# Layer 1 experts: the loads of an expert wait for the adds of the expert eight places ahead of it

## What is computed

```
logits = x @ gate_w.T;  probs = softmax(logits);  4 experts of 32 are picked per token
buf[e, slot] = x[token]                       # up to 256 rows for each of 32 experts
gu = buf @ w_gate_up[e]                       # (256 x 256) @ (256 x 256)
expert_out = (silu(g) * u) @ w_down[e]        # (256 x 128) @ (128 x 256)
routed[token] += expert_out[e, slot] * gate   # scatter-add, 256 rows per expert
out = x + tanh(g_ffn) * (routed + shared expert)
```

## Time and profile before

| | us |
|---|---|
| median of the runs | 1098.03 |
| the profiled execution | 1095.2 |
| its span | 1093.2 |
| TensorE matmul busy | 909.6 |
| GpSimd busy | 541.6 |
| first add instruction of the stage starts | 922.30 |
| last add instruction of the stage starts | 1050.72 |

### The profile page before, as it was taken

The page is one execution under the profiler, slowest core; times in us unless marked ns, Lnnn a source line. Parts: engine busy times, 40 slices in busy tenths (PEclk is TensorE's granted clock), DMA queues, the critical chain, the costliest instruction groups (busy, mean ns, idle before and its releaser), DMA issues. The chain is left out here.

```text
span 1093.2 us, 18614 instructions
## 1 busy us (share of the span) xinstructions
PE 909.6 (83%) x5465; PEld 764.5 (70%) x5465; DVE 663.3 (61%) x2223; ACT 459.7 (42%) x1721; POOL 541.6 (50%) x592
## 2 busy tenths in 40 slices
PE   4998759999999698888538999999999979999920
PEld 3673437787877487777437888998898866888710
DVE  4603035777777466565438899999999963444431
ACT  1313652322322135544326577777777741222200
POOL 1300123455555625555534765565556553677861
PEclk8878988888988699999869999999999989999965
DMA  9521884668776967676499963623413004999689
GB/s 307 185 91 49 246 237 126 161 189 226 237 207 197 248 205 220 213 244 208 130 267 199 222 162 102 230 77 127 136 40 111 12 16 135 264 256 241 70 192 156
DMA packets 163957, 189.71 MB, mean 174 GB/s; under 512 B 16035, under 2 KB 145209, under 8 KB 163858
## 3 DMA queue, kind: packets, MB, share of 16 engines
q1 hardware_dynamic: 112882, 121.87, 38.1%
q0 software_dynamic: 33792, 46.46, 19.7%
q10 hardware_dynamic: 17184, 20.19, 5.4%
HBM read 96.19 MB, written 103.63 MB: 183 GB/s over the span
## 5 line engine op out<-in xcount | busy, mean ns | idle before, releaser
L1794 ACT ACTIVATE att<-bank,mx 128x77 f32<-128x77 f32 x512 | 160.2, 355 | 18.8 <-DVE mx L1875 17.2
L1742 POOL DMA_INDIRECT slots_d<-rows,place x128 | 130.1, 1017 | 71.8 <-DVE place L1963 40.9
L1794 ACT ACTIVATION_READ_ACCUMULATOR att<-bank,mx 128x1 f32 x512 | 121.3, 237 | 0.0
L960 POOL DMA_INDIRECT y_d<-rows,targets x78 | 80.9, 1037 | 70.5 <-DVE rows L1291 47.3
L2061 PE MATMUL bank<-vwo_hi,attT_hi 128*128 128x256 f32 x320 | 94.3, 295 | 3.0 <-DMA vwo_lo<-vwo_lo_d 2.0
L2062 PE MATMUL bank<-vwo_lo,attT_hi 128*128 128x256 f32 x320 | 91.4, 286 | 0.0
L2063 PE MATMUL bank<-vwo_hi,attT_lo 128*128 128x256 f32 x320 | 91.1, 285 | 0.0
L2061 PE MATMUL bank<-wqk_hi,xa_hi 128*128 128x462 f32 (+1 forms) x192 | 76.2, 397 | 6.3 <-DVE xa_lo L1880 6.3
L1781 ACT ACTIVATE attT_hi<-bank 128x512 fp32r<-128x512 f32 x64 | 39.0, 610 | 83.0 <-PE bank L2101 83.0
L927 POOL DMA_INDIRECT slots_d<-rows,place x64 | 63.8, 996 | 15.9 <-issue 15.6
L1313 PE MATMUL bank<-wd_hi,act_hi 128*128 128x256 f32 (+1 forms) x206 | 69.8, 339 | 1.9 <-POOL act_lo L921 1.1
(11 more groups left out here) (302 smaller groups left out, 2715.8 us busy)
## 6 DMA issues: line engine op xcount, KB each, us to landing
expert_gate_up<-in_wgu SPq DMA_DIRECT2D x40, 256.0 KB
rows<-slots_d SPq DMA_DIRECT2D x39, 260.0 KB
slots_d<-zrow SPq DMA_DIRECT2D x8, 1168.0 KB
expert_rows<-slots_d SPq DMA_DIRECT2D x32, 292.0 KB
x_res<-y_d POOLq DMA_DIRECT2D x14, 512.0 KB, 12.1
expert_down<-in_wd SPq DMA_DIRECT2D x40, 128.0 KB
wqk_d<-wqk SPq DMA_DIRECT2D x32, 154.0 KB, 3.7
vwo_d<-vwo SPq DMA_DIRECT2D x16, 308.0 KB
```

The costliest lines, as they stand in the source:

```text
L960: pool.indirect_dma_start(y0_d, bass.IndirectOffsetOnAxis(ap=tgt0[:, s % NY0, b:b + 1], axis=0), y_rows(s, b), None, bounds_check=T * K0 - ...
L1742: pool.indirect_dma_start(slots_d, bass.IndirectOffsetOnAxis(ap=place[:, n % 3, k:k + 1], axis=0), rows[:, n % 3, :], None, bounds_check=S ...
L1794: last = act.activation(att[:, par, h * S:(h + 1) * S], bank[:, a, i * S:(i + 1) * S], ACT.Exp, scale=-1.0, bias=mx[:, par, h:h + 1], accu ...
```

## The change

SyncE waits for one more counter before it issues the three DMAs of expert e (from 8 on): the adds of expert e-8 must have landed.

```diff
                         sp.wait_ge(targets, e - NB + 1)
                         sp.wait_ge(g_down, e - NB + 1)
                         sp.wait_ge(g_y, e - NB + 1)
+                        sp.wait_ge(added4[(e - NB) % 2], 16 * BLK * ((e - NB) // 2 + 1))
                         load_rows(e)
```

## The result

The changed kernel takes 1105.58 us in the median (20 runs, 1097.33 to 1108.55) beside 1099.23 us for the one before (20 runs on the same chips, 1093.68 to 1107.65). The ratio is 1.0038, with a 95% interval of 1.002 to 1.0055. A second comparison on another chip gave 1.0041 (1.0005 to 1.0078). Forecast was 1091.9 us, and the range ended at 1102.

The account below looks back on a forecast made before the run. GpSimd's adds were taken to bound the last stage, losing 10.6 us to loads delaying landings; pace 3.89 over 25 experts saves 6.1 us: 1098.0 - 6.1 = 1091.9 us. Range: from 1087.4, with a us for spread, to 1102.

Parts of the forecast that it names:

- The wait's own cost: On SyncE in the last stage: the added wait is one semaphore test on an otherwise idle engine, taken as 0.
- TensorE's rows: In the last stage: later loads make TensorE 2.3 us late for its rows, which costs nothing at the end.
- the cover of 11 us: At the kernel's end: 11.0 us between VectorE's last shared chunk and first sum; earlier adds take 6, TensorE's delay 2.3.
- no clock would be lost: TensorE in the last stage: only small holes expected, granted clock stays 1.00, cost taken as 0.
- 0.3 us between landing and start: GpSimd's adds: gap between the awaited landing and the next add's start, leaving some 1.4 us of landing delay free.
- the same position as in these two rows: Loads of the last stage: they would meet second adds as at experts 8 and 15, giving mean w 5.93.
- w: GpSimd's adds: time from an expert's second add to the first add two experts on; 5.57 us or less loses nothing.
- the pace of 3.89: GpSimd's adds under the change: 3.89 us per expert, (1.86 + 5.93) / 2, bringing expert 31 6.1 us earlier.
- rival b: GpSimd's adds are never held: pace 3.71, 10.6 us earlier, 1087.4 us; the wait regulates itself; chance 0.22.
- (c): Lockstep in the last stage: loads always meet the next expert's second add; 6.1 us later, 1104.1 us; chance 0.13.
- 25 paces: GpSimd's adds from expert 2 to 27: the stretch loads can disturb under the change, in place of 20 paces before.
- (a): Last stage: thinner loads disturb adds as much, but 25 paces, not 20; 2.6 us later, 1100.7 us; chance 0.25.

Follow-up runs that it names:

- no_loads: The change with the loads of experts 8 to 31 left out, these experts using the data of experts 0 to 7; ratio 0.9883 to the kernel before.
- four_sums_change: The change with adds going to four tensors in turn in place of two, the extra sums left out of the output; ratio 0.9891 to the kernel before.
- after_second_issue: The change, but each load waits for a count raised behind the second add of expert e-8, not a landing; ratio 0.9945 to the kernel before, 0.9949 again.
- pairs_on_purpose: As after_second_issue, but the load of an even expert waits one expert longer, so it is asked for with the next; ratio 1.0120 to the kernel before.
- at_first_issue: The change, but each load waits for a count raised just ahead of the first add of expert e-8, not a landing; ratio 1.0049 to the kernel before.

## Why the prediction was wrong

**What bounds the kernel:** right. The adds, 10.6 us lost to the landing of e-2, loads as the cause, TensorE ahead: no_loads and four_sums_change show each of them.

**The wait's own cost, TensorE's rows, the cover of 11 us:** right in effect. TensorE came later than I had it (holes up to 2.7 us, 11.0 us in all, in place of 2.3) and its clock dipped, and neither reached GpSimd, as all 18.6 us are in the 12 holds and the outputs were there well ahead. That no clock would be lost was wrong, but without effect. My 0.3 us between landing and start was too small: the landing counted at 940.91 releases the add that starts at 941.75, 0.84 us. So 5.57 - 3.83 - 0.84 = 0.9 us of an add's delay is free, not 1.4.

**The step that failed** is "the same position as in these two rows. Mean w is 5.93", from which the pace of 3.89 was worked out. Measured: w = 7.11 and a pace from expert 2 to 27 of (1047.95 - 936.60) / 25 = 4.45. There are two errors in it. The first is the value. It was the mean of two rows, w 5.57 and 6.29, with loads 0.77 and 0.43 us before the second add, carried over to a load 0.1 us behind it. The trace of before has seven experts with a load within 0.55 us of the second add, of 1, 2, 3, 4, 15, 17 and 18; their w is 6.29 to 7.51, 6.87 in the mean, and the 6.29 that I took is the lowest. (Six of them have another load some 3 us ahead, a little closer than the 3.7 to 4 us that I expected.) Expert 2 is one of them: load 11 is issued at 932.31, its second add starts at 932.52, and expert 4 starts 7.51 us later, in the timelines of SyncE and GpSimd before:

```profile
932.31 0.37 SPq L1672 DMA_DIRECT2D expert_rows<-slots_d  x1
...
932.52 1.54 POOL L1756 DMA_INDIRECT acc_d<-expert_out,target_rows  x1 [0.30 <-issue]
...
940.03 1.55 POOL L1756 DMA_INDIRECT acc_d<-expert_out,target_rows  x1 [0.54 <-issue]
```

With 6.87 my sum would have given a pace of 4.37 and 5.8 us later, close to what came. The second error is that the position was worked out for one landing at its undisturbed time, and then kept for all of them. The new wait ties loads to landings that the loads themselves delay, and I took this loop as calming ("a wait that regulates itself", rival b). It does the opposite: it gathers the loads in pairs. With w = 7.11 in my sum expert 31 comes at 930.67 + 25 x 4.49 + 14.84 = 1057.8, 8.9 us later than before, beside the 8.0 that D shows.

**The rivals.** (c), lockstep, had 0.13 and is what happened in sign and size: 6.1 us later by its own price, 4 to 6 measured. That the size fits is in part luck, since it was a half-way value and its mechanism was half right: the loads do lock onto the adds, in pairs and some 2.6 and 1.1 us ahead of the second add of every odd expert, not singly on each. It is also right that 25 paces are covered in place of 20, as (a) has it, but the price per load is no constant: (D - 111.5) / 24 is 0.3 us in after_second_issue, 0.4 to 0.5 before, 0.6 to 0.8 in the change, and 0.9 in pairs_on_purpose. The Trainium skill (DMA: Bandwidth & Descriptors, Queues, rings and completion order) says that an engine drains one packet of a queue, typically 9 to 17 descriptors, and then turns to the next. An estimate from it: with each of the profile's packets of the earlier trace rows, 51 ns in the mean, taken for a descriptor, 17 of them are 0.9 us for an add, 1.8 for two. Measured, the adds of expert 5 land 7.2 us after the second is started (951.90 to 959.11) in place of 3.8, 3.4 us late. So a typical packet does not explain the size of the delay, and no run here shows how the engines divide their time between the queues.

**The range** should have reached beyond (c). I priced it half way between break-even and the worst row, called it improbable by two rows, and ended the range 2 us short of its price.

## What to carry to other kernels

A load that is tied to the completion of transfers which it slows down is part of a loop, and such a loop can bunch the loads; look at the distances between successive loads, not at their mean rate. A count raised behind the issue of the second add kept them apart here, while counts raised ahead of the adds gave pairs again, so the place has to be tried and not only the kind of signal. Where a share of DMA time near 1 goes with a stall, take away the wait behind the stall before believing in a lack of throughput: here four tensors in place of two let the same bytes through without loss in this stage. And a price read from two rows of a varying quantity is a guess; the other rows of that position were in the trace, and they said 6.87. Last, where a wait is for several semaphores, look up when each of them was met before believing the releaser that is named.

## What the runs showed of the hardware

- GpSimd goes through semaphore increments ahead of indirect DMAs that it has not started: in at_first_issue by at least 2.9 us (926.23 against 929.13).
- From the last count of an add's landing to the start of the add that waits for it 0.84 us pass (940.91 to 941.75 in the change, and ten more like it). An add whose second instruction is undisturbed lands 3.6 to 4.2 us after its start (no_loads, experts 1 to 26); beside a pair of loads it took 5.3 to 7.8.
- Adds and loads together reach a DMA share of 1.05 and 244 GB/s at an undisturbed pace of 3.71 us per expert.
- D of one kernel moves between executions, 121.9 and 124.1, 129.9 and 126.6, 119.0 and 119.6, and the start of the stage by 12 us, so single profiles of such a kernel say nothing of a few microseconds in the whole, and inside the stage only of more than some 3 us.
